# Eight-head attention: in every second item, ScalarE writes the mask into the PSUM bank and TensorE adds the turned score onto it

## What is computed

```
scores = einsum('bhnd,bhmd->bhnm', q, k) / sqrt(16)
scores = where(mask, -inf, scores)        # mask: adjacency == 0 (second layer: symmetrised, with the diagonal)
w      = softmax(scores, axis=-1)
out    = einsum('bhnm,bhmd->bhnd', w, v)
```

## Time and profile before

| what | before |
|---|---|
| runs shown | 4680.42 us median (4680.33 to 4680.91) |
| profiled execution: time / span | 4680.85 us / 4679.1 us |
| TensorE busy over the span | 3567.5 us (76%) |
| VectorE / ScalarE / GpSimd busy | 2859.8 (61%) / 2003.5 (43%) / 1805.2 us (39%) |
| L1217, mask matmuls | x1024 |
| L1339, exponentials | x1024, mean 601 ns |

### The profile page before, as it was taken

How to read it: one execution, slowest core, us unless ns; L and a number is a source line. 1 busy time by engine, 2 the same in 40 slices (tenths; PEclk the granted TensorE clock), 3 DMA queues, 4 the chain that set the end, 5 groups by cost and what they waited for, 6 DMA issues and landing times. The chain is left out here.

```text
span 4679.1 us, 81278 instructions
## 1 busy us (share of the span) xinstructions
PE 3567.5 (76%) x24077; PEld 2156.5 (46%) x24077; DVE 2859.8 (61%) x10923; ACT 2003.5 (43%) x4994; POOL 1805.2 (39%) x2183
## 2 busy tenths in 40 slices
PE   3999996666666638999988777639947698884994
PEld 1333333444444423333335556627736555552663
DVE  5666665555555566666649787842247767773444
ACT  1666663322222215656643226524426555551221
POOL 3444430000000015455538224764545535553445
PEclk7999996555555559999999888869978999996997
DMA  4333326800000013333300012224443100002445
GB/s 127 110 109 109 105 69 280 338 0 0 0 0 0 0 53 110 110 109 102 101 13 0 2 37 73 74 68 142 149 139 105 46 1 20 18 21 75 129 129 163
DMA packets 237345, 378.36 MB, mean 81 GB/s; under 512 B 24833, under 2 KB 157057, under 8 KB 228673
## 3 DMA queue, kind: packets, MB, share of 16 engines
q1 hardware_dynamic: 218688, 337.44, 22.8%
q0 software_dynamic: 18432, 38.31, 2.3%
HBM read 210.70 MB, written 164.95 MB: 80 GB/s over the span
## 5 line engine op out<-in xcount | busy, mean ns | idle before, releaser
L1436 DVE CUSTOM_DVE_ANT_0 mha_seen<-mha_score,mha_mask 128x512 f32<-128x512 f32 x1024 | 686.5, 688 | 455.9 <-PE mha_score L1207 452.9
L1339 ACT ACTIVATE mha_prob<-mha_turned 128x512 f32<-128x512 f32 x1024 | 609.0, 601 | 489.9 <-PE mha_turned L1218 459.8
L1592 PE MATMUL lstm_gates<-lstm_h_part,lstm_w_part 128*128 128x16 f16 x4608 | 277.7, 179 | 328.1 <-DVE lstm_h_part L1807 324.8
L3109 POOL DMA_INDIRECT expert_rows<-expert_y,expert_target x320 | 306.6, 958 | 359.5 <-DVE expert_y L3255 154.6
L1207 PE MATMUL mha_score<-mha_k_rows,mha_q_rows 96*128 96x512 bf16 x1024 | 398.2, 391 | 57.0 <-DMA mha_k_rows<-split_rows 28.8
L1592 PEld LDWEIGHTS lstm_gates<-lstm_h_part,lstm_w_part 128*128 128x128 f16 x4608 | 216.5, 107 | 481.0 <-DVE lstm_h_part L1807 475.8
L1217 PE MATMUL mha_turned<-mha_maskT,core_ident_bf 128*128 128x512 bf16 x1024 | 392.8, 384 | 4.0 <-ACT mha_prob L1339 3.5
L1218 PE MATMUL mha_turned<-mha_q_rows,mha_k_rows 99*128 99x512 bf16 x1024 | 391.0, 382 | 0.0
L1539 POOL TENSOR_TENSOR core_mid<-lstm_hist,lstm_per_unit 128x128 f32 x64 | 29.4, 460 | 887.1 <-DVE lstm_hist L1808 887.1
L1679 ACT ACTIVATE lstm_act<-lstm_gates 128x48 f32<-128x48 f32 x512 | 108.0, 211 | 428.6 <-PE lstm_gates L1592 428.6
L3147 PEld LDWEIGHTS expert_out_ps<-expert_w,expert_hid 128*128 128x128 f32 (+1 forms) x2240 | 262.4, 191 | 38.7 <-issue 33.0
(11 more groups left out here) (554 smaller groups left out, 8830.6 us busy)
## 6 DMA issues: line engine op xcount, KB each, us to landing
routed_rows<-lstm_blank SPq DMA_DIRECT2D x66, 1056.0 KB, 26.6
core_params<-adj SPq DMA_DIRECT2D x32, 1024.0 KB, 5.8
gat_adj_raw<-adj SPq DMA_DIRECT2D x32, 1024.0 KB, 5.4
mha_q_rows<-split_rows SPq DMA_DIRECT2D x64, 384.0 KB, 4.3
mha_k_rows<-split_rows SPq DMA_DIRECT2D x64, 384.0 KB, 5.3
expert_x<-routed_rows SPq DMA_DIRECT2D x80, 264.0 KB, 2.8
expert_w<-weights SPq DMA_DIRECT2D x80, 256.0 KB, 3.5
combine_pair<-expert_rows SPq DMA_DIRECT2D x32, 512.0 KB, 4.6
```

The costliest lines, as they stand in the source:

```text
L1339: act.activation(prob[:, n % RING, :], turned[n % 2][:, :], ACT.Exp, scale=-1.0).then_inc(S["prob_ready"], 1)
L1436: dve.tensor_tensor_reduce(seen[n % 2][:, :], score[n % 2][:, :], mask[1 - s][:, t, :], 1.0, 3e38, ALU.add, ALU.min, low[g][:, t, j:j + 1] ...
L1592: return pe.matmul(out, w[:, g * P:(g + 1) * P], h_part[:, part, :], start=False, stop=stop, skip_group_check=True)
L3109: pool.indirect_dma_start(out=core.y_rows[NUMBER][:, :], out_offset=bass.IndirectOffsetOnAxis(ap=target[q][:, t:t + 1], axis=0), in_=y_buf ...
```

## The change

For even items TensorE no longer adds the mask. ScalarE copies the mask tile (bf16, in SBUF) into the whole of bank `turned[0]` (f32) ahead of the product (`fill`), and the product is added onto it with `start=False`. The fill of item n+2 stands in ScalarE's program right behind the exponential of item n, which is the last reader of that bank, and waits for the end of it (`prob_ready`); the fill of a graph's item 0 stands behind the exponential of item 30 of the graph before. The product waits for `filled`. Odd items stay as they are. Two matmuls at the start of a stage (`marked`) write both banks once, so that a later matmul without `start` adds to what the bank holds. `take_mask` waits for `filled` as well as for `turned_done`, since the fills read `maskT`.

```diff
--- before.py
+++ after.py
@@ -941,6 +941,8 @@
     ROWS = BLOCKS * head_dim
     ITEMS = 2 * 4 * T
     RING = 8
+    EVERY = 2
+    FILLS = ITEMS // EVERY
     FIRST, LAST = -2, B
     with ExitStack() as ctx:
         m = Mem(nc, ctx, tag)
@@ -978,7 +980,7 @@
                  "mask_ready", "mask_turned", "joined", "join_chain", "maskT_ready", "score_done", "score_taken", "low_chain",
                  "low_split", "row_in_psum", "row_ready", "shift_out", "shift_in0", "shift_in1", "turned_done", "prob_ready", "pv_done",
                  "v_done", "v_ready", "oT_ready", "back_done", "ctx_chain", "ctx_ready", "ctxt_in_psum", "ctxT_ready", "attn_done",
-                 "base_chain", "base_ready", "out_taken", "tail", "saved"]
+                 "base_chain", "base_ready", "out_taken", "tail", "saved", "filled", "marked"]
         S = {n: m.sem(n) for n in names}
         wq, wk, wv, wo = (core.param(k, w + tag[-1]) for w in ("wq", "wk", "wv", "wo"))
         bv, bo = (core.param(k, w + tag[-1]) for w in ("bv", "bo"))
@@ -1151,6 +1153,9 @@
         def _(pe):
             pe.wait_ge(core.params_in[k], 16)
             pe.wait_ge(S["const_set"], 8)
+            for bank in turned:
+                ones = rows[1][0][ROWS:ROWS + 3, 0, :]
+                pe.matmul(bank[:, :], ones[:, 0:P], ones, start=True, stop=True).then_inc(S["marked"], 1)
 
             def rows_in(x):
                 need(pe, "xn_ready", x + 1)
@@ -1213,10 +1218,13 @@
                     need(pe, "maskT_ready", 2 * b + 2)
                 if n % 16 == 0:
                     need(pe, f"shift_in{g}", 16 * (b + 1))
-                need(pe, "prob_ready", ITEMS * b + n - 1)
-                pe.matmul(turned[n % 2][:, :], core.ident_bf[:, :], maskT[s][:, u, :], start=True, stop=False)
+                if n % EVERY == 0:
+                    need(pe, "filled", FILLS * b + n // EVERY + 1)
+                else:
+                    need(pe, "prob_ready", ITEMS * b + n - 1)
+                    pe.matmul(turned[n % 2][:, :], core.ident_bf[:, :], maskT[s][:, u, :], start=True, stop=False)
                 pe.matmul(turned[n % 2][:, :], rows[1][s][0:ROWS + 3, h, u * P:(u + 1) * P], rows[0][s][0:ROWS + 3, h, :],
-                          start=False, stop=True).then_inc(S["turned_done"], 1)
+                          start=False, stop=True, skip_group_check=n % EVERY == 0).then_inc(S["turned_done"], 1)
 
             def values(b, s, quad):
                 g, u = quad // 4, quad % 4
@@ -1320,8 +1328,17 @@
                 need(act, "attn_done", x)
                 act.copy(ctxT[:, :], misc[0][:, :]).then_inc(S["ctxT_ready"], 1)
 
+            def fill(x, s, n):
+
+                if n == 0:
+                    need(act, "maskT_ready", 2 * x + 2)
+                    need(act, "marked", 2)
+                need(act, "prob_ready", ITEMS * x + n - 1)
+                act.copy(turned[n % 2][:, :], maskT[s][:, n // 4 % 4, :]).then_inc(S["filled"], 1)
+
             def take_mask(x, s, i):
                 need(act, "turned_done", ITEMS * (x - 1))
+                need(act, "filled", FILLS * (x - 1))
                 out = maskT[s][:, 2 * i:2 * i + 2, :]
                 if sym:
                     need(act, "mask_ready", x + 1)
@@ -1337,6 +1354,10 @@
                         if n % 4 == 0:
                             need(act, "pv_done", 8 * b + n // 4 - 1)
                         act.activation(prob[:, n % RING, :], turned[n % 2][:, :], ACT.Exp, scale=-1.0).then_inc(S["prob_ready"], 1)
+                        if (n + 2) % EVERY == 0 and n + 2 < ITEMS:
+                            fill(b, s, n + 2)
+                    if n + 2 == ITEMS and has_s:
+                        fill(b + 1, 1 - s, 0)
                     if prep and n in (3, 5):
                         take_qk(b + 2, n // 2 - 1)
                     if n == 4 and tail:
```

## The result

The changed kernel takes 4734.72 us (median of four runs, 4729.54 to 4737.30) against 4680.66 for the kernel before beside it: ratio 1.0111, 95% interval 1.0099 to 1.0123. It is slower by 54 us. Forecast were 18 us, and 4722 as the upper end of the range. The profiled execution took 4732.63 us with a span of 4730.6, 51.5 more than before's span.

A forecast was written before the change was run, and what follows sets the result against it. TensorE, 95% and 94% busy in the attention stages, was taken as the bound, with ScalarE already bounding items 3 to 7. 15.4 us for take_qk periods plus 2.2 for last graphs, 17.6 on 4680.85, gave 4698 us; range 4666 to 4722.

The forecast's parts named there:

- the engines and the places: Attention stages: TensorE the engine to relieve; leads built mid-period are spent on ScalarE at take_ctx, take_mask and take_qk.
- the clock: Rival: TensorE loses its granted clock in the new gaps, ending over 4722 us; chance 0.02.
- the price of a fill: ScalarE without a gap: a 0.58 us copy, pitch 0.46, signal 0.05; one fill adds 0.62 us.
- the cycle of the even bank: Pair of items without score items between, last graph: cycle grows from 1.30 to 1.70 us as the fill replaces the matmul.
- the dear rival: Rival on ScalarE's self-wait: at 0.18 a fill costs 0.17 us more, 0.85 a period, 4722 in all; chance 0.15.
- The 6 us: If PSUM copies were some 0.04 us shorter than SBUF ones, the whole would come out some 6 us lower, near 4692.
- step 4: One first-stage period walked through: lead 0.44 at item 12, about 0.1 at project_out; project_v 0.8 us later, period 40.7.
- VectorE's wait at item 28: Second stage: item 28's score waits 0.48 us for VectorE; about 0.5 more lead lasts, so the period grows 0.3 us.
- the sum: Both stages: 14 x 0.8 + 14 x 0.3 = 15.4 us, plus 2.2 for last graphs, together 17.6 us.
- the last graphs: Last graph of each stage: a quad's first pair grows 0.40, its second half shrinks about 0.26; 2.2 us in all.
- The two periods ahead of the last graphs: Period before each stage's last graph, without prep or take_qk: counted at nothing, quads at +0.1 and others at -0.2.
- The first rival: TensorE stays the bound, faster: about 4666 us, 4569 with nothing given back, if a fill costs under about 0.45; chance 0.20.

The follow-up runs named there:

- the kernel that only loads ScalarE: Against the changed kernel: all mask matmuls kept, the 512 copies go to a spare SBUF tile nobody reads; ratio 1.0195 to the kernel before.
- the one that only unloads TensorE: Against the changed kernel: even items have neither fill nor mask matmul, their mask left out of the result; ratio 0.9876 to the kernel before.
- the late fill: Against the changed kernel: the fill of item n+2 stands behind the exponential of item n+1 instead of item n; ratio 1.1279 to the kernel before.
- six picked fills: Against the changed kernel: only items 0, 4, 12, 16, 20 and 24 filled; ratio 0.9986, and 0.9978 when run again, to the kernel before.
- eight well chosen fills: Against the changed kernel: only items 0, 2, 4, 12, 16, 20, 24 and 26 filled; 4769.10 us, ratio 0.9969 to the kernel before.

## Why the prediction was right in direction and wrong in size

**Right: the engines and the places.** TensorE is the busiest engine, ScalarE holds it up at `take_row`, `take_ctx` and `take_mask`, and the leads of the middle are spent there. The waits came where they were forecast: 1.98 and 1.89 us ahead of `project_v` (1.5 to 2), TensorE at 87% (86), even products waiting for the fill, though for 0.04 to 0.47 us in the full graphs and not 0.4 to 0.6. That the load on ScalarE outweighs the relief of TensorE is shown by the kernel that only loads ScalarE (+92 us, a third of it the clock's) against the one that only unloads TensorE (-58).

**Right: the price of a fill.** Its duration is 0.589 us (taken 0.58) and the cycle of the even bank 1.70 (forecast 1.70). The wait for the own exponential is 0.03 (taken 0.05), far from the 0.18 of the dear rival, which falls. The pitch is 0.52 to 0.53 where I took 0.46, the pitch of a copy out of PSUM, so a fill costs ScalarE (0.63 - 0.49) + 0.52 = 0.66 to 0.68 and not 0.62. The stretch from item 3 to the end of `take_row` grew by 1.07 us, forecast 0.95.

On the destination, the copy of the same tile took 589 ns into PSUM and 618 into SBUF. The Trainium skill, "ScalarE: Activation LUTs" (Step-by-step: what each stage is for), states that ScalarE writes faster to PSUM than to SBUF; these two groups agree, by 29 ns, where the prediction's estimate from the Trainium skill, "Perfetto Trace Analysis" (Optimizing Scalar/DVE Operations), was some 0.04 us. The 6 us that the prediction made of that estimate are not there: the copy's pitch is 0.524 us into PSUM and into SBUF alike.

**Wrong: step 4, the lead at items 8 to 16.** This is the step that failed. I had the product of item 12 run 0.44 us ahead and carried the lead on to `take_ctx`, looking at TensorE and ScalarE alone. To have 0.1 left at `project_out` behind a copy that stands 0.62 later, exponential 16 had to lead by 0.7; the walk says so nowhere. These are the leads against before, worked out from the starts behind `project_v` (323.91 after, 314.53 before):

| checkpoint | before | after | lead | forecast |
|---|---|---|---|---|
| product item 12 | 5.82 | 5.42 | +0.40 | +0.44 |
| score item 14 | 7.91 | 7.73 | +0.18 | |
| product item 16 | 10.59 | 10.20 | +0.39 | +0.7, as `project_out` needs |
| `project_out` | 12.22 | 12.48 | -0.26 | +0.1 |
| `turn_mask` | 20.89 | 20.76 | +0.13 | +0.45 |
| product item 30 | 26.43 | 26.60 | -0.17 | +0.2 |
| exponential item 3 | 33.71 | 34.05 | -0.34 | +0.15 |
| next `project_v` | 39.81 | 41.22 | -1.41 | -0.8 |

Up to item 12 the forecast holds. At item 16 a third of a microsecond is missing. The score of item 14 was held back by VectorE before the change too, with TensorE idle for 0.34 us:

```profile
321.72 0.38 PE L1218 MATMUL mha_turned<-mha_q_rows,mha_k_rows 99*128 99x512 bf16 x1
322.44 0.39 PE L1207 MATMUL mha_score<-mha_k_rows,mha_q_rows 96*128 96x512 bf16 x1 [0.34 <-DVE mha_low L1436]
```

I had not put that row on my list. In the changed kernel the product stands at 331.10, so the score could start 0.22 later, at 331.32; VectorE holds it until 331.64. These 0.32 us are what is missing at item 16 and, to 0.04, at `project_out` (0.36), and again at `turn_mask` (0.32), because TensorE streams without a gap from that score to the product of item 16. The kernel without any mask for even items shows the wait for what it is: TensorE comes earlier, and the wait only grows, to 0.64 us. No run took VectorE's wait away by itself, so its share is worked out from these starts. From `turn_mask` to the exponential of item 3 another 0.17 is lost, in the stretch with `take_mask` and fills 28, 30, 0 and 2, and 0.12 in the row of items 3 to 7 (1.07 for 0.95). From the last two rows, the missing 0.61 us per period is 0.49 of lead and 0.12 of that chain. The kernel without fills 6 and 8 bears the split out: with the chain gone its period is still 0.34 us longer than before, the lead of -0.34 in the table.

In the second stage I had seen VectorE's wait at item 28 and given 0.5 us for it. The period ended at the same 41.3 us as in the first stage, so it grew by 0.89 where I had 0.3. It is the same step: in the second stage the leads at `project_out` and `turn_mask` are -0.26 and +0.13 again, exponential 3 leads by 0.18 where the forecast needs 0.65, and without fills 6 and 8 the period is 0.18 shorter than before, so that the chain costs 1.07 here too. Together this term is 32.2 us where the sum had 15.4.

**Wrong: the clock.** I gave its loss a chance of 0.02 because the mean of 86% busy seemed ample. But the mean hides a place with 1.9 us of idle time, 2.1 of 4 us busy, behind which the clock fell. The fall cost six graphs some 1.4 us each, 8.4 in all, forecast nothing; with seven useless matmuls in that place no full graph had it. Up to 1.64 us of idle time there (the fills at the first items of the quads) brought no drop. It isn't the length of the one idle time alone either: with the late fill the clock fell behind 4 us with 2.00 busy whose idle times were 0.96 and 1.04.

The 1.6 us of the first graph lie behind a start with half the clock in both kernels: in the windows from 108 to 112 and 112 to 116 us the granted clock was 0.50 and 0.75, before 0.67 and 1.00, so it came back later. That is not shown to be the change's. The kernel with six picked fills has it in one of its two profiled executions (+1.9 us) and not in the other (-0.5).

**Wrong: the last graphs.** Forecast 2.2 us for both, measured 6.0. ScalarE's timeline of the first stage's last graph, the counterpart of the earlier trace rows:

```profile
745.76 1.08 ACT L1356 ACTIVATE mha_prob<-mha_turned 128x512 f32<-128x512 f32 x2 [0.32 <-PE mha_turned L1226]
...
749.52 1.15 ACT L1356 ACTIVATE mha_prob<-mha_turned 128x512 f32<-128x512 f32 x2
750.70 0.59 ACT L1337 CAST mha_turned<-mha_maskT 128x512 f32<-128x512 bf16 x1
751.22 1.14 ACT L1356 ACTIVATE mha_prob<-mha_turned 128x512 f32<-128x512 f32 x2
...
753.30 1.08 ACT L1356 ACTIVATE mha_prob<-mha_turned 128x512 f32<-128x512 f32 x2 [0.32 <-PE mha_turned L1226]
```

Two quads take 7.54 us (745.76 to 753.30), 3.77 each, 0.45 more than the 3.32 of before and not 0.14 (over all eight quads the mean is 0.38). The first pair is as forecast: 1.70 us for 1.30 (749.52 to 751.22). The second half was to shrink from 2.02 to 1.76, by the matmul taken away; it takes 2.08 (751.22 to 753.30). TensorE's timeline shows why:

```profile
751.34 0.39 PE L1226 MATMUL mha_turned<-mha_q_rows,mha_k_rows 99*128 99x512 bf16 x1 [0.57 <-ACT mha_turned L1337]
751.66 1.07 PE L1236 MATMUL mha_o<-mha_prob,mha_v 128*32 128x512 f32 x8
752.66 0.39 PE L1225 MATMUL mha_turned<-mha_maskT,core_ident_bf 128*128 128x512 bf16 x1
```

From the even product (751.34) to the odd exponential (753.30) TensorE has the values, the odd item's mask and its product. The even item's mask was never in this stretch: it stood ahead of the even product, where the fill stands now. So there was nothing to take away there. The two periods ahead of the last graphs, counted at nothing, cost 1.9.

**The terms together.** `take_qk` periods 32.2 (forecast 15.4), clock in six graphs 8.4 (0), last graphs 6.0 (2.2), periods ahead of them 1.9 (0), and 1.6 in the first graph that may be no part of the change. The first rival, TensorE staying the bound, falls: its condition was a fill under 0.45 and it costs 0.66 to 0.68. Yet part of it holds for a choice of places: with six or eight well chosen fills the stages get 13 to 16 us shorter.

## What to carry to other kernels

When work moves from a busy engine to one that looks idle on average, walk the period and look up every wait of every engine in it, those of 0.3 us on a third engine too: such a wait takes back any lead that reaches it. The same instruction can be free in one place and cost 0.5 us in another (here fills 6 and 8, 1.07 together; -1.8 us in all for eight fills a graph at the quads' first items, +37.1 for eight at the third ones), so try the places apart before the idea is given up. Look at the stretches in which the edit leaves TensorE half idle and not only at its mean load. When an instruction is moved to another place in an engine's program, follow what it now stands behind: the fill one item later joined two chains into one.

## What the runs showed of the hardware

- An instruction on ScalarE that waits by semaphore for the one ahead of it starts 0.03 us behind its end, which makes 0.63 us in place of the 0.49 of two exponentials back to back; on GpSimd the same wait took 0.18.
- ScalarE's copy of a bf16 tile from SBUF has a shorter duration into PSUM than into SBUF (589 and 618 ns) but the same pitch, 0.52 us; an f32 copy out of PSUM has 0.46 to 0.48. So the destination made no difference to what the copy costs a full engine, and the length of a row doesn't tell it.
- Idle time of 1.9 to 2.0 us in a stretch that was half busy brought the granted clock down in six of 28 graphs, in six again in a second profiled execution and in seven with the last graphs changed; 2.0 to 2.1 us did so in 17 of 28 (copies into SBUF). 1.0 us (before), 1.5 to 1.6 us (fills at the first items) and 0.47 us (filled up) never did.
- The same kernel took 4680.7, 4678.0, 4786.7 and 4785.9 us in four sets of runs. The kernel with six picked fills ran on chips of both kinds: its attention stages agree within 2.3 us there (-6.7 and -9.0, -4.4 and -8.9), the 2.3 us being the first graph, so that the 108 us lie elsewhere in the program.
